# A graph-attention kernel: 18 instead of 17 tiles of gathered rows a layer fetched by SyncE, self-loop loads spread out, layers' ends reordered

## The reference

```python
h = relu(layernorm(x))
for l in range(2):
    xn = layernorm(h) * g1 + b1
    xp = xn + xn @ Wpos + bpos + deg * Wdeg + bdeg
    q, k, v = xp @ Wq + bq, xp @ Wk + bk, xp @ Wv + bv        # 8 heads of 16
    att = clip(sum_d(q[dst] * k[src]) / 4, -50, 50)           # one value per edge and head
    alpha = softmax of att over the edges (and the self loop) of each dst
    h = h + segment_sum(v[src] * alpha, dst) @ Wo + bo
    h = h + gelu(layernorm(h) * g2 + b2 @ W1 + b1) @ W2 + b2
return x + h
```

## Time and profile before

| | |
|---|---|
| median of 3 runs | 2121.98 us (2121.76 to 2126.15) |
| profiled execution | 2121.11 us, span of its instructions 2119.3 us |
| busy of the span | PE 65%, DVE 81%, ACT 42%, POOL 72% |
| mean granted TensorE clock | 0.818 of full speed |
| DMA | 290.12 MB, mean 137 GB/s |

### The profile page before, as it was taken

The page is one execution under the profiler, slowest core; times in us unless marked ns, Lnnn a source line. Parts: engine busy times, 40 slices in busy tenths (PEclk is TensorE's granted clock), DMA queues, the critical chain, the costliest instruction groups (busy, mean ns, idle before and its releaser), DMA issues.

```text
span 2119.3 us, 44962 instructions
## 1 busy us (share of the span) xinstructions
PE 1380.0 (65%) x8158; PEld 1214.5 (57%) x8158; DVE 1708.2 (81%) x5168; ACT 882.5 (42%) x2159; POOL 1522.9 (72%) x1620
## 2 busy tenths in 40 slices
PE   4965566666666666666766656656666667666666
PEld 4655565655556565555556655555566556555565
DVE  8768899889888888888866778787787778787876
ACT  8433353443534343443443334334343434334344
POOL 6177777777777777777727777777777777777773
PEclk8979887788978788887877778888886877789778
DMA  3464454545444444444434444444444444444442
GB/s 90 127 173 148 147 153 154 153 135 152 139 146 130 146 139 146 129 143 143 134 100 135 140 139 137 134 139 143 139 133 140 142 134 135 143 140 136 135 141 63
DMA packets 135156, 290.12 MB, mean 137 GB/s; under 512 B 36900, under 2 KB 70368, under 8 KB 134880
## 3 DMA queue, kind: packets, MB, share of 16 engines
q0 software_dynamic: 77088, 206.02, 34.0%
q10 hardware_dynamic: 18784, 55.33, 7.9%
q1 hardware_dynamic: 39008, 25.91, 4.1%
HBM read 275.44 MB, written 8.38 MB: 134 GB/s over the span
## 4 chain that ended last, share of the span: by engine, by line
POOL 40%; issue 20%; DVE 12%; PE 8%; DMA 8%; ACT 6%; ACTq 3%; SPq 3%; DVEq 1%
POOL kvr L889 40%; DMA kvr<-kv_table,srcidx 7%; DVE agg L1857 3%; PE bank L1177 3%; PE bank L1190 3%; DVE kvr L1478 2%; ACTq L1436 2%; ACT apart L1401 2%; SPq L750 2%; ACT onehotT L1405 1%; DVE msg L1844 1%; DVE onehot L1809 1%; ACTq L1434 1%; ACT L1354 1%; DVE prod L1817 1%
## 5 line engine op out<-in xcount | busy, mean ns | idle before, releaser
L889 POOL DMA_INDIRECT kvr<-kv_table,srcidx x1564 | 1484.7, 949 | 533.3 <-issue 457.3
L1177 PE MATMUL bank<-q,onehotT 128*128 x3320 | 596.2, 336 | 685.1 <-DVE prod L1817 329.8
L1177 PEld LDWEIGHTS bank<-q,onehotT 128*128 128x128 f32 x3320 | 507.8, 234 | 792.9 <-issue 790.0
L1190 PE MATMUL bank<-msg,onehot 128*128 128x136 f32 x3320 | 603.5, 341 | 0.1
L1190 PEld LDWEIGHTS bank<-msg,onehot 128*128 128x128 f32 x3320 | 564.8, 249 | 0.6 <-DVE msg L1844 0.3
L1857 DVE TENSOR_TENSOR agg<-agg,bank 128x136 f32 x1624 | 469.4, 289 | 52.6 <-PE bank L1190 48.6
L1442 ACT ACTIVATE bank<-attc 128x32 f32<-128x32 f32 x404 | 80.9, 200 | 1013.5 <-DVE attc L1838 947.4
L1817 DVE TENSOR_TENSOR prod<-kvr,bank 128x512 f32<-128x512 f32 (+1 forms) x404 | 269.7, 667 | 279.3 <-DMA kvr<-kv_table,srcidx 241.7
L1401 ACT ACTIVATE apart<-relT,minus_p 128x512 bf16<-128x512 bf16 x416 | 293.9, 707 | 0.6 <-DMA relT<-rel_table 0.2
L1809 DVE TENSOR_TENSOR onehot<-bank,rel 128x512 f32<-128x512 f32 x416 | 282.6, 682 | 0.5
L1844 DVE TENSOR_TENSOR msg<-kvr,bank 128x512 f32<-128x512 f32 (+1 forms) x404 | 267.8, 663 | 16.6 <-ACT bank L1442 16.2
(11 more groups left out here) (224 smaller groups left out, 781.9 us busy)
## 6 DMA issues: line engine op xcount, KB each, us to landing
rowkv<-kv_table SPq DMA_DIRECT2D x4352, 1.0 KB
relT<-rel_table ACTq DMA_DIRECT2D x102, 512.0 KB
act_rowkv<-kv_table ACTq DMA_DIRECT2D x1792, 1.0 KB
kvr<-kv_table,srcidx POOLq DMA_INDIRECT x1564
loop_kv<-kv_table SPq DMA_DIRECT2D x25, 128.0 KB
kv_table<-qkv SPq DMA_DIRECT2D x25, 128.0 KB
kv_table<-onehot SPq DMA_DIRECT2D x8, 256.0 KB, 2.2
w<-weights SPq DMA_DIRECT2D x2, 840.0 KB, 7.5
```

The lines of the kernel that those rows point to most:

```text
L889: pool.indirect_dma_start(kvr[:, n % RING, j, :], None, kv_table[l], bass.IndirectOffsetOnAxis(ap=srcidx[:, step:step + 1], axis=0)).then_ ...
L1177: mm = pe.matmul(bank[2][:, j * D:(j + 1) * D], onehotT[:, m % OHT, j, :], q[:, bass.ds(ranks[j + h], 1), :].rearrange("p a c -> p (a c)") ...
L1190: mm = pe.matmul(sum_ps(n, k), onehot[:, m % OH, j, :], msg[:, n % 2, j, :], start=(m, j) == of[0], stop=(m, j) == of[-1])
```

## The change

SP takes 18 tiles a layer: from group 12 on every eleventh group in layer 0, and from group 9 on in layer 1 (before: 17, from group 19 on in both). Where the first slots of a tile's fetch would lie ahead of the layer, their parts are issued together in slot 0. The self-loop loads of layer 0 stand every 20 slots instead of every seven. At the layers' ends, `DVE_O` of chunk 7 goes from slot 197 to 198, its second layer norm and the first half of its feed-forward move on by one slot, and chunk 6's `DVE_LOOP` goes from slot 198 to 204. DVE loads the ranks for the next slot ahead of the guard, instead of at the slot's start.

```diff
-ROWED = [tuple(range(first + ROW_SLOTS + ROWS_LEAD, GROUPS - 1, ROW_SLOTS)) for first in (5, 5)]
+ROWED = [tuple(range(first, GROUPS - 1, ROW_SLOTS)) for first in (12, 9)]
...
-    return 24 + 7 * c
+    return 24 + 20 * c
...
-LATE_DVE = {DVE_LN2: -5, DVE_Y: 5, DVE_LN1: 6, DVE_QKV: 12, DVE_SCORES: 13, DVE_LOOP: 15}
-LATE_PE = {PE_LN2: -4, PE_FF: -3, PE_FF + 1: -1, PE_Y: 3, PE_LN1: 7, PE_QKV: 9}
-LATE_ACT = {ACT_STD2: -6, ACT_LN2: -4, ACT_FF: -2, ACT_FF + 1: -1, ACT_STD1: 5, ACT_LN1: 7, ACT_Q: 13, ACT_LOOP: 14}
+LATE_DVE = {DVE_O: -5, DVE_LN2: -4, DVE_Y: 5, DVE_LN1: 6, DVE_QKV: 12, DVE_SCORES: 13, DVE_LOOP: 15}
+LATE_PE = {PE_LN2: -3, PE_FF: -2, PE_FF + 1: -1, PE_Y: 3, PE_LN1: 7, PE_QKV: 9}
+LATE_ACT = {ACT_STD2: -5, ACT_LN2: -3, ACT_FF: -2, ACT_FF + 1: -1, ACT_STD1: 5, ACT_LN1: 7, ACT_Q: 13, ACT_LOOP: 14}
...
+LAST_EARLY = {DVE_LOOP: BASE[-1] + 1}
...
-            moved = [part for part, slot in early.items() if slot == at]
+            moved = [part for part, slot in early.items()
+                     if (LAST_EARLY[part] if c == LATE - 1 and early is EARLY_DVE and part in LAST_EARLY else BASE[c] + slot) == s]
...
-                        if 0 <= s - (g - ROWS_LEAD - ROW_SLOTS) < ROW_SLOTS:
-                            fetch_rows(l, g, s - (g - ROWS_LEAD - ROW_SLOTS))
+                        part = s - (g - ROWS_LEAD - ROW_SLOTS)
+                        for k in range(0 if s == 0 else part, part + 1):
+                            if 0 <= k < ROW_SLOTS:
+                                fetch_rows(l, g, k)
...
+            next_ranks = []
+
             def edge_iteration(n):
...
-                ranks = read_ranks(ENG.DVE, n - 2) if g >= 2 else None
+                ranks = list(next_ranks)
...
                     edge_guard(n)
                     add(3)
+                    next_ranks[:] = read_ranks(ENG.DVE, n - 1)
                     return
...
                     edge_onehot(n + 2)
+                if g >= 1:
+                    next_ranks[:] = read_ranks(ENG.DVE, n - 1)
                 edge_guard(n)
...
-                        for k in (n - 2, n - 1):
-                            ranks = read_ranks(ENG.DVE, k)
+                        last_ranks = read_ranks(ENG.DVE, n - 1)
+                        for k, ranks in ((n - 2, next_ranks), (n - 1, last_ranks)):
```

## The result

The changed kernel takes 2132.76 us (median of 5 runs, 2130.63 to 2136.57), the kernel before 2123.02 us in the same comparison: ratio 1.0043, 95% interval 1.0033 to 1.0054, slower. Run once more on another chip it was 1.0056 (1.0043 to 1.0069). The profiled execution is that of 2130.63 us, with a span of 2128.9 us, 9.6 us above before's.

A forecast was written before the change was run, and what follows sets the result against it. POOL's gather stream plus each layer's end bounds the kernel; with the change, SP's serial rows decide layer 0. Span 2119.3 + 14.0 - 1.6 = 2131.7, plus 1.8 outside and 0.9 to the median: 2134.5 us stated, range 2126 to 2141.

The forecast's parts named there:

- The sum: Whole kernel: span 2119.3 + 14.0 - 1.6 = 2131.7 us, with time outside the span and the runs' median 2134.4, stated as 2134.5.
- SP's price: SP in layer 0: one row costs 0.395 us of issuing, so one tile more costs 50.6 us.
- The landing: Group 199 in layer 0: rows land 4.1 us after the last issue at 1090.0, so at 1094.1; DVE waits 13.9 us.
- +0.1: Layer 0's end behind group 199's row product: added work and removed waits net to +0.1 us.
- This is the term that decides: SP's one tile more in layer 0: with the end behind it, layer 0 ends 14.0 us later, bounds 9.0 to 16.9.
- a check on the wait: DVE, eleven slots from group 188 to 199 in layer 0: about 49.4 us of its own, arriving at 1093.
- Layer 1: Layer 1: one gather less and no wait for chunk 7's projection gain 0 to 3.2 us, taken as 1.6.
- A: SP in layer 0: rows come in time if a tile takes under about 49.7 us; kernel faster, 2117.3 us; chance 0.12.
- B: Layer 0: SP's lag reaches POOL through its ring of eight groups, holding it 30 us in sum; 2144 us; chance 0.10.
- C: Layer ends gain 3.3 us in layer 0, 3.2 in layer 1, rows landing at the lower bound; 2124.5 us; chance 0.06.
- the rule of the Trainium skill: Row DMAs on SP: spreading issue over engines only saves issue time, usually small beside the DMA; would end at 2117.3 us.

The follow-up runs named there:

- rest_alone: The changed kernel with SP's 17 tiles from group 19 on in both layers, as before: 2119.85 us, ratio 0.9984 to the kernel before.
- no_last_tile: The changed kernel without layer 0's last tile, group 199 all from POOL: 2131.58 us, ratio 1.0035 to the kernel before.
- after_again: The changed kernel run once more, unaltered, on another chip: 2131.43 us, ratio 1.0056 to the kernel before.
- tiles_alone: The kernel before with the change's 18 tiles (from groups 12 and 9 on) and nothing else of it: 2134.24 us, ratio 1.0057.
- ends_alone: The kernel before with the layers' ends reordered as in the change and nothing else: 2116.86 us, ratio 0.9989.
- loops_by_act: The changed kernel with ScalarE instead of SP issuing layer 0's nine self-loop loads: 2113.56 us, ratio 0.9963 to the kernel before.
- short1: The changed kernel leaving out one row of 128 in each of layer 0's last 15 tiles: 2126.64 us, ratio 1.0035 to the kernel before.
- short2: The changed kernel leaving out two rows of 128 in each of layer 0's last 15 tiles: 2122.89 us, ratio 1.0019 to the kernel before.
- short4: The changed kernel leaving out four rows of 128 in each of layer 0's last 15 tiles: 2114.92 us, ratio 0.9979 to the kernel before.
- late18: The changed kernel with layer 0's 18 tiles at groups 28, 38, ... 198: 2160.53 us, ratio 1.0192 to the kernel before.

## Why the prediction was right, point by point

**The sum.** The forecast was 12.5 us on top of 2122.0; measured are 9.7 on top of 2123.02. In the profiled executions layer 1 begins 12.1 us later than before (14.0 predicted) and takes 2.5 us less (1.6 predicted).

**SP's price was right.** 18 tiles took SP from 134.69 to 1089.43 almost without a pause (1.9 us of waits), 954.7 us against 903.4 for 17: 51.3 us for a tile, 50.6 predicted. `load_x0` ended at 1108.0 and was covered, as predicted. DVE waited 78.8 us for rows in all (about 80 predicted) and, in the stretch of the earlier trace rows, never for gathers. The reason given for the 0.395 us was incomplete: 0.225 and 2.17 / 32 make 0.293. From one row's issue to the next it is 0.32 us in the trace of before, with a register move of 0.029 us and gaps between, and 0.32 + 0.07 make 0.39.

**The landing was mis-sized.** I took 4.1 us from issue to landing, the one row product that waited in the trace before. At group 199 the product starts 1.1 us behind the last issue. So it stands at 1090.57 and not at 1094, 10.4 us later than the 1080.2 of before in place of 13.9. SP had also begun 1.3 us earlier in this execution (134.69, before 135.97).

**Behind it the end is not +0.1.** From that product to layer 1's first gather it takes 35.1 us, and 33.35 before (1113.55 less 1080.2): +1.75. The granted clock from 1089 to 1125 was 0.83, and 0.90 at before's end, but most of the 1.75 shows without that. At a granted clock of 0.90, it takes from the product of group 199's gathers to that first gather 35.21 us in `rest_alone` (1074.62 to 1109.83), 34.97 in `no_last_tile` and 33.94 before. So about 1.0 to 1.3 us go with the reordered ends, which the sum had at +0.1. This miss and that of the landing have opposite signs and cancel in part.

**"This is the term that decides" was half the cause.** The prediction priced the loss at the one tile more. It noted that DVE would come from group 188 at its own pace at 1093 (it came at 1089.73: 48.3 us for eleven slots, 49.4 predicted), but treated that as a check on the wait. `no_last_tile` shows that this arrival is a cause of its own: taking the tile away gives back nothing that can be told from zero, because the other 17 have been moved seven groups forward against an SP that starts no earlier. DVE and the rows reach group 199 within 0.32 us of each other. So a sum over one of the two causes gave about the right time, and nothing in the prediction says why they should meet; that is luck.

**Layer 1** is 2.5 us shorter in the profile, 1.6 predicted (0 to 3.2). Group 9's product stands at 1180.94 and waits for no row there; in `after_again` it waits 1.1 us. Whether the gain is the tile's or the ends' is not settled: layer 1 takes 1005.0 us in `tiles_alone`, 1002.5 in `ends_alone` and 1006.3 in `loops_by_act`, and the clock at its end moves it by more.

**The rivals.** A (rows in time) asked for a tile under 49.7 us. The mean tile of layer 0 was 50.2 us in `short1`, 49.9 in `short2` and 49.2 in `short4` (rows fetched over 18, times 0.395): late, 3 us over the floor, at the floor. The limit fits, and the kernel is on the wrong side of it. B (POOL's ring) did not happen: POOL waited 5.2 us for messages in layer 0 (10.4 before), never more than the 0.3 us that also lie between two gathers without a wait. In `late18`, where waits at one tile reached 11.6 us, it waited 32.4, up to 6.6 at once. C is not needed, but part of it is there: `ends_alone` is 2.4 us faster (0.4 to 4.2) where nothing is late.

**On the rule of the Trainium skill** (DMA: Bandwidth & Descriptors, "Issuing engines are not separate DMA queues") the trace disagrees for this kernel on how much issue matters. Issue time was the bound: moving 25 DMAs and their address loads to another engine turned 1.0043 and 1.0056 into 0.9963, 17 to 20 us, and took 17.7 us out of layer 0.

## What to carry to other kernels

An engine that issues many small DMAs in series is a resource with a budget like any other: count what it issues, in us of its own time, against the deadline of each piece, not against its share of waits. Moving every deadline forward can cost as much time as the whole change, as it did here, and taking only the last piece away repaired nothing while the pieces ahead were late too. An engine that issues loads and stores in one order can lose its head start again: in `late18` SP stood 17.1 us at a store whose data was not there yet.

## What the runs showed that I had not expected

The same end of layer 1 takes up to 3.7 us more or less between executions, and TensorE's granted clock differs with it. The last 24 us of `ends_alone`, 24 us of the changed kernel and 27 us of `short1` (from, to and length in us, busy time and count of PE, PE's weight loads, DVE, ACT and POOL, granted clock, DMA share, GB/s):

```profile
2089.00:2113.00 24.00, 13.81 (x85) 10.77 (x85) 11.44 (x39) 11.42 (x23) 0.43 (x1) 0.99 0.07 20
```
```profile
2105.00:2129.00 24.00, 16.23 (x85) 13.36 (x85) 11.58 (x39) 11.45 (x23) 0.44 (x1) 0.86 0.07 20
```
```profile
2100.00:2127.00 27.00, 19.62 (x85) 15.46 (x85) 11.52 (x39) 11.70 (x23) 0.36 (x1) 0.75 0.06 17
```

For 85 matmul records each PE is busy for 13.8, 16.2 and 19.6 us. In the chain of the changed kernel and of `short1` (where it is five lines lower) the last product of the feed-forward's first half shows the two levels, 2.4 and 1.2 GHz:

```profile
2120.81 1.99 PE bank L1127 x8
```
```profile
2117.52 3.78 PE bank L1132 x8
```

These matmuls stand in the chain at a layer's end. The clock is not all of it: from POOL's last gather to the end of the span it takes 24.4 us in `ends_alone` at 0.99 and also in the changed kernel at 0.85, but 28.0 in `short1`, and as long in `short4`, `loops_by_act` and `late18`, at 0.76 in all four. Effects of one or two us in the whole time, as the tile of layer 1, disappear in that. The length of layer 0 between two gathers scatters less.
